# Softmax denominators inverted straight from PSUM and spread by a transpose, with a new table of slots for the attention phase

## The reference

```python
x = L0_attn_q
x = x + 0.5 * _L0_ffn_ref(_layernorm(x), theta, phi, theta_noise, phi_noise)
x = x + _L0_attn_ref(_layernorm(x), Wq, Wk, Wv, Wo)
x = x + 0.5 * _L0_ffn_ref(_layernorm(x), theta, phi, theta_noise, phi_noise)
x = x + 0.5 * _L1_ffn_ref(_layernorm(x), gate_w, gate_b, expert_w, expert_b)
x = x + _L1_attn_ref(_layernorm(x), W_in, A_log, dt_bias, B_norm_bias, C_norm_bias, W_out)
x = x + 0.5 * _L1_ffn_ref(_layernorm(x), gate_w, gate_b, expert_w, expert_b)
```

```python
xq = rope(q @ Wq); xk = rope(kv @ Wk); xv = kv @ Wv
xk, xv = repeat(xk, 2), repeat(xv, 2)
scores = jax.nn.softmax(xq @ xk * scale, axis=-1)
out = (scores @ xv).transpose(0, 2, 1, 3).reshape(batch, seq_len, -1)
return out @ Wo
```

## Time and profile before

| what | value |
|---|---|
| median of 3 runs | 2895.76 us (2888.0 to 2897.27) |
| the profiled execution | 2892.05 us, span of its trace 2890.3 us |
| granted TensorE clock, mean over the span | 0.938 |
| PE matmul busy | 2428.1 us (84%) |
| DVE busy | 1918.0 us (66%) |
| ACT busy | 1465.3 us (51%) |
| POOL busy | 1257.4 us (44%) |
| DVE maxima, L327 | 1024 times, 680 ns each |
| ACT exponentials, L464 | 1024 times, 596 ns each |
| POOL pair sums, L533 | 384 times, 1277 ns each |

### The profile page before, as it was taken

The page is one execution under the profiler, slowest core; times in us unless marked ns, Lnnn a source line. Parts: engine busy times, 40 slices in busy tenths (PEclk is TensorE's granted clock), DMA queues, the critical chain, the costliest instruction groups (busy, mean ns, idle before and its releaser), DMA issues. The chain is left out here.

```text
span 2890.3 us, 41583 instructions
## 1 busy us (share of the span) xinstructions
PE 2428.1 (84%) x14724; PEld 1163.0 (40%) x14724; DVE 1918.0 (66%) x4634; ACT 1465.3 (51%) x2794; POOL 1257.4 (44%) x1104
## 2 busy tenths in 40 slices
PE   2788988898889889988898837999999999997578
PEld 1223332332333233323332224666666666665333
DVE  4776777677777777777777213666666666665477
ACT  2266656655665666566655625555555555552000
POOL 3365556555655655565553412233223223322233
PEclk8799999999999999999999968999999999998789
DMA  2212111111121112111111010000000000000011
GB/s 101 64 32 47 39 36 36 46 34 41 30 52 34 27 44 49 31 31 47 44 27 26 5 45 5 8 12 12 8 9 12 9 11 8 9 5 9 26 51 44
DMA packets 73293, 87.01 MB, mean 30 GB/s; under 512 B 9216, under 2 KB 59520, under 8 KB 72960
## 3 DMA queue, kind: packets, MB, share of 16 engines
q1 hardware_dynamic: 73088, 84.37, 11.6%
HBM read 21.16 MB, written 12.58 MB: 12 GB/s over the span
## 5 line engine op out<-in xcount | busy, mean ns | idle before, releaser
L327 DVE TENSOR_REDUCE mS<-ps 128x1 f32<-128x512 f32 x1024 | 676.2, 680 | 319.4 <-PE ps L670 314.9
L464 ACT ACTIVATE pr<-ps 128x512 f32<-128x512 f32 x1024 | 583.5, 596 | 394.6 <-PE ps L654 383.5
L533 POOL TENSOR_TENSOR prs<-pr 128x512 f32<-128x512 f32 x384 | 484.3, 1277 | 336.5 <-ACT pr L464 336.5
L670 PE MATMUL ps<-kst,qst 96*128 96x512 f16 x1024 | 406.7, 398 | 60.7 <-DVE mS L327 48.3
L654 PE MATMUL ps<-qst,kst 97*128 97x512 f16 x1024 | 400.6, 395 | 47.9 <-ACT pr L464 45.5
L692 PE MATMUL ps<-pr,vt 128*32 128x512 f32 x2048 | 286.1, 632 | 0.1
L654 PEld LDWEIGHTS ps<-qst,kst 97*128 97x128 f16 x1024 | 99.5, 98 | 412.6 <-ACT pr L464 275.2
L537 POOL TENSOR_TENSOR terms<-terms 128x512 f32<-128x512 f32 x128 | 162.2, 1267 | 138.6 <-DVE terms L320 138.6
L320 DVE TENSOR_TENSOR terms<-ps,rope 128x512 f32<-128x512 f32 x256 | 172.5, 676 | 28.0 <-POOL lo L542 22.0
L1396 ACT ACTIVATE m_rl<-m_ps,posb 128x512 f32<-128x512 f32 x128 | 86.1, 684 | 192.2 <-PE m_ps L1682 192.2
L670 PEld LDWEIGHTS ps<-kst,qst 96*128 96x128 f16 x1024 | 101.5, 99 | 197.6 <-DVE mS L327 129.1
(11 more groups left out here) (250 smaller groups left out, 4489.9 us busy)
## 6 DMA issues: line engine op xcount, KB each, us to landing
qst<-hi SPq DMA_DIRECT2D x128, 128.0 KB, 2.4
kst<-hi SPq DMA_DIRECT2D x128, 128.0 KB, 2.4
qst<-lo SPq DMA_DIRECT2D x64, 128.0 KB, 2.4
kst<-lo SPq DMA_DIRECT2D x64, 128.0 KB, 2.4
x<-in_q SPq DMA_DIRECT2D x16, 256.0 KB, 2.7
rope<-in_rope SPq DMA_DIRECT2D x1, 4096.0 KB, 12.2
x<-yold SPq DMA_DIRECT2D x16, 256.0 KB, 2.3
m_x<-x SPq DMA_DIRECT2D x16, 256.0 KB, 2.8
```

The costliest lines, as they stand in the source:

```text
L327: v.tensor_reduce(mS[:, b % 2, t, s:s + 1], ps[:, 2 + n % 2, :], AX, ALU.max).then_inc(S["s_read"], 1)
L464: a.activation(pr[:, s % 2, g, :], ps[:, g % 2, :], ACT.Exp, scale=ATT_SCALE).then_inc(S["exp"], 1)
L533: g.tensor_tensor(prs[:, c, :], pr[:, 0, c, :], pr[:, 1, c, :], ALU.add).then_inc(S["prs"], 1)
L670: mm(ps[:, 2 + n % 2, :], qst[0:3 * DH, h, P * t:P * t + P], kst[0:3 * DH, h, :], start=True, stop=True).then_inc(S["s"], 1)
```

## The change

In the division, the ACT copy is gone: the first transpose reads bank 7 of PSUM itself, and it raises the semaphore `den`, so PE may write the bank again when DVE has read it. The copy that repeated the inverses is gone too: the second transpose reads `inv` with each element repeated 32 times by its access pattern. The multiply gets a wait for the numerators (`o`). The three parts move from slots 24 to 26, 40 to 42 and 56 to 58 to slots 21 to 23, 37 to 39 and 53 to 55; the last group keeps slots 0 to 2. And sixteen numbers of the table change: the four value projections, aggregation of the first norm, both evacuations, ffn, squares, top two and count of the gate, and five of the 16 projections.

```diff
--- before.py
+++ after.py
@@ -71,18 +71,11 @@
 
 ATTENTION_AT = {
 
-
-    "values": (1, 3, 8, 9), "output": 4, "x2": 4,
-
-    "stats1": 5, "aggr1": 9, "xn1": 11, "turn1": 16, "evac1": 16, "ffn": 17, "squares": 21, "ffn_b": 22,
-    "squares_b": 22, "sqrt": 25, "resid": 25, "stats2": 27, "aggr2": 29, "xn2": 31, "turn2": 36, "evac2": 36,
-    "gate": 37, "gate_in": 37, "gate_top": 38, "gate_count": 44,
-
-    "project": (37, 38, 39, 40, 41, 43, 44, 46, 47, 48, 50, 51, 54, 57, 59, 60), "high_lag": 3, "low_lag": 2,
-    "denominators_lag": 3,
-
-
-    "maxima": 5,
+    "values": (0, 1, 7, 8), "output": 4, "x2": 4, "stats1": 5, "aggr1": 8, "xn1": 11, "turn1": 16, "evac1": 17,
+    "ffn": 18, "squares": 19, "ffn_b": 22, "squares_b": 22, "sqrt": 25, "resid": 25, "stats2": 27, "aggr2": 29,
+    "xn2": 31, "turn2": 36, "evac2": 35, "gate": 37, "gate_in": 37, "gate_top": 41, "gate_count": 45,
+    "project": (37, 38, 39, 40, 41, 42, 45, 46, 47, 49, 50, 51, 53, 56, 59, 60), "high_lag": 3, "low_lag": 2,
+    "denominators_lag": 3, "maxima": 5,
 }
 
 HEAD_GROUPS = 6
@@ -337,17 +330,21 @@
                 def divide(b, j, part):
 
                     if part == 0:
+                        if j < NG - 1:
+                            dve.wait_ge(S["dn"], 2 * ((NG - 1) * b + j + 1))
+                        else:
+                            dve.wait_ge(S["dd"], NT * (b + 1))
+                        ins = v.transpose(denT[:, :], ps[:, 7, :])
+                        ins.then_inc(S["den"], 1)
                         dve.wait_ge(S["den"], NG * b + j + 1)
-                        dve.wait_ge(S["dve"], mark(v.transpose(denT[:, :], den[:, :])))
                         div_done[0] = mark(v.reciprocal(inv[:, :], denT[:, 0:SEQ:32]))
                     if part == 1:
                         dve.wait_ge(S["dve"], div_done[0])
-                        dve.wait_ge(S["dve"], mark(v.tensor_copy(
-                            denT[:, :].rearrange("p (b i) -> p b i", i=32),
-                            inv[:, :].rearrange("p (b o) -> p b o", o=1).to_broadcast([P, SEQ // 32, 32]))))
-                        div_done[0] = mark(v.transpose(den[:, :], denT[:, :]))
+                        div_done[0] = mark(v.transpose(
+                            den[:, :], inv[:, :].rearrange("p (b o) -> p b o", o=1).to_broadcast([P, SEQ // 32, 32])))
                     if part == 2:
                         dve.wait_ge(S["dve"], div_done[0])
+                        dve.wait_ge(S["o"], NG * b + j + 1)
                         v.tensor_tensor(oT[:, j, :], oT[:, j, :], den[:, :], ALU.mult).then_inc(S["norm"], 1)
 
 
@@ -360,8 +357,8 @@
                             maximum(maximum_at(i, q))
                         if guard_at(i, q) is not None:
                             guard_row(guard_at(i, q))
-                        if is_att(i) and s % NG == 2 and s > NG and t < 3:
-                            divide(i - 2, s // NG - 1, t)
+                        if is_att(i) and s % NG == 1 and s > NG and t:
+                            divide(i - 2, s // NG - 1, t - 1)
                         if is_old(i) and q < 3:
                             divide(i - 3, NG - 1, q)
                         if is_old(i) and q == AT["x2"]:
@@ -440,15 +437,6 @@
                         act.wait_ge(S["wo"], b)
                     a.copy(oT[:, j, :], ps[:, 6, :]).then_inc(S["o"], 1)
 
-                def denominators(b, j):
-                    if j < NG - 1:
-                        act.wait_ge(S["dn"], 2 * ((NG - 1) * b + j + 1))
-                    else:
-                        act.wait_ge(S["dd"], NT * (b + 1))
-                    if NG * b + j:
-                        act.wait_ge(S["norm"], NG * b + j)
-                    a.copy(den[:, :], ps[:, 7, :]).then_inc(S["den"], 1)
-
                 def exponentials(b, s, g):
                     head = HEADS * b + s
                     if g == 0 and head >= 2:
@@ -475,8 +463,6 @@
                                 a.copy(vt[:, t, :], ps[:, 5, :]).then_inc(S["v"], 1)
                             if s and s % NG == 0 and g == 3:
                                 numerators(i - 2, s // NG - 1)
-                            if s > NG and s % NG == 1 and g == 2:
-                                denominators(i - 2, s // NG - 1)
                         for part in range(4):
                             if q == AT["xn1"] + part:
                                 normalise(i, lambda t: x8[:, t, :], 1, part)
@@ -505,7 +491,6 @@
                             high(i, high_at[q])
                     if is_att(i):
                         numerators(i - 2, NG - 1)
-                        denominators(i - 2, NG - 1)
 
             @block.gpsimd
             def _(pool):
```

## The result

The changed kernel takes 2824.88 us (median of 4 runs, 2820.94 to 2825.83); the kernel before took 2892.53 us beside it (2888.0 to 2897.27). The ratio is 0.976, with a 95% interval of 0.9742 to 0.9778: 2.4% faster. The profiled span fell from 2890.3 to 2824.0 us, by 66.3, at a mean granted clock of 0.944 instead of 0.938. One execution in all that follows, one of the four of e4_actcopy, took 3216.14 us at a mean clock of 0.73; the ratios leave it out.

A forecast was written before the change was run, and what follows sets the result against it. PE was taken as nearest to a bound, yet idle 12 us per iteration, waiting for other engines. Gains of 0.6 + 0.6 + 2.1 + 0.4 = 3.7 us per full iteration, 54 us in all, gave 2840 us, range 2810 to 2880.

The forecast's parts named there:

- the likeliest case: The forecast proper, all four stages gaining as summed: 2824 to 2858 us, chance 0.62.
- T1: Slots 5 to 16, first norm: aggregation one slot earlier, with two maxima ahead of it instead of three; gain 0.6 us.
- T2: Slots 22 to 36, ffn to second norm: the division's multiply leaves DVE's run behind the root; gain 0.6 us.
- T3: Slots 38 to 52, rotary products: shorter division lets POOL's chain start sooner and take 16.0 us; gain 2.1 us.
- T4: Slots 0 to 4, last inverse ahead of the output projection: DVE's copy leaves the chain; gain 0.4 us.
- ACT's copy at nothing: Removing ACT's copy of 0.584 us was priced at gain 0; 0.58 at most in T1 to T4 if ACT were late.
- B: Rival: POOL or ACT takes T3, which then brings 0.1 us; 26 us gained, 2866 us; chance 0.13.
- C: Rival: T3 gives up all its DVE waits, 3.9 us, and the clock comes back; 2799 us; chance 0.07.
- D: Rival, slower: PE's waits at slots 27 and 28 merge, half clock reaches into T3; 2903 us; chance 0.07.
- E: Rival: a new transpose is slow, 1.42 us in place of 0.70; 24 us gained, 2868 us; chance 0.06.
- D's rate: Each us of half clock reaching into T3 would cost about half a us.
- waits for terms: Sign: PE's waits for DVE products, 50.3 us before, fall below 30 us in 13 iterations.

The follow-up runs named there:

- e4_actcopy: Changed kernel with ACT's copy of the denominators put back, the first transpose reading that copy; 2849.99 us, 0.9839 of the kernel before.
- e2_table: New table of slots with the division of the kernel before (both copies, old division slots); 2887.35 us, 0.9973 of the kernel before.
- e5_first_late: Changed kernel with only the first group's division moved back from slots 21 to 23 to slots 24 to 26; 2837.94 us, 0.9821.
- e11: Changed kernel with the gate's choices back in slot 38 and PE's gaps filled by repeated score matmuls; 2831.13 us, 0.9792.
- e10: Changed kernel with one number put back, the gate's choices in slot 38 instead of 41; 2868.35 us, 0.9921 of the kernel before.
- e1: Changed kernel's division (no copies, new slots) with the table of slots of the kernel before; 2878.91 us, 0.9938.
- e9: New division with the table of the kernel before, except the gate's choices in slot 41, not 38; 2847.11 us, 0.9846.
- e3_dvecopy: Changed kernel with DVE's spreading copy put back ahead of the second transpose, which reads the copy; 2863.61 us, 0.9886.
- the filled kernels: Kernels in which PE repeats score matmuls where it stood idle, e11 and i4_fill; 2831.13 and 2812.19 us.
- i4_fill: Changed kernel with the eight score matmuls of slots 26, 27 and 30 to 35 issued three times; 2812.19 us, 0.9719.

## Why the prediction came out as it did

The forecast was 2840 with a range of 2810 to 2880; 2824.9 lies in it, at the lower edge of the likeliest case's own 2824 to 2858. The mechanism was right, and the steady part of the sum was right to 0.05 us. That closeness is in part luck: T1 and T2 together gave 1.06 us and not 1.2, T3 and T4 a little more than forecast.

- **T1, 0.6 predicted.** The first shift stands 7.97 us behind the residual, 8.56 before: 0.59. e2_table shows the same 0.59 alone. At the second ffn 0.46 of it is left.
- **T2, 0.6 predicted, 0 for squares and evacuations.** 0.60 more at the second shift. e5_first_late undoes it and loses 0.60. The squares and evacuations were not tried singly. For the squares PE's rows bear the argument out: behind the second ffn it waited 1.05 us for POOL's pair sum and 0.72 for ACT before, and now waits 0.75 and 1.02, the same 1.77 in all. In the changed kernel:

```profile
727.91 1.07 PE L686 MATMUL ps<-prs,ones 128*32 128x512 f32 x8 [0.75 <-POOL prs L518]
730.00 0.39 PE L639 MATMUL ps<-qst,kst 97*128 97x512 f16 x1 [1.02 <-ACT pr L452]
```

- **T3, 2.1 predicted.** 36.0 to 33.8: 2.2, at full clock. POOL's chain took exactly the 16.0 us worked out, and the multiply fell in POOL's pause and took 0.67, the better of the two cases. One step was wrong all the same: "the table's other shifts (gate_top 38 to 41, ...) leave DVE's sum the same". The sum stays, and yet with gate_top at 38 T3 takes 35.1 us at full clock (e11) and 37.3 with the clock that it then gets (e10). My chain from maximum to product silently had the choices out of slot 38 already; I used the new place and priced it at nothing. Undoing it costs 43 of the 68 us, some 20 by the order and the rest by the clock, and without it the new division brings 0.6% (e1) in place of 1.5% (e9).
- **T4, 0.4 predicted.** The stretch from the last division's first transpose to the output projection fell from 3.83 to 3.38, 0.45. The value projections' wait of 0.24 is hidden, as said.
- **The sum.** 3.7 per iteration against 3.72 between the cleanest iterations, 48.1 against 48.4 in 13.
- **ACT's copy at nothing.** The stages came out right without it, so it held where the copy stood; e4_actcopy shows that it does not hold in the new order.
- **What was missing, 12 us of 66.** Iterations 16 and 17 gave 8.5 and not 3.2; the clock in the 13 iterations gave 3.6 and the phases that the change leaves alone 3.4, which is luck. For iteration 16 I took T1, T2 and T4 and left T3 out because it has no projections. But it has the gate, its choices and counts, and the division.

The kernel before in iteration 16, DVE and then PE in the timeline behind the gate sum of 1546.27:

```profile
1548.40 1.28 DVE L59 CAST gif<-gix 128x8 f32<-128x8 uint32 x1
...
1550.47 0.51 PE L670 MATMUL ps<-kst,qst 96*128 96x512 f16 x1 [1.95 <-DVE mS L327]
1560.95 0.61 PE L670 MATMUL ps<-kst,qst 96*128 96x512 f16 x1 [2.82 <-DVE mS L327]
```

The window of its 18 us from that gate sum on:

```profile
1546.27:1564.27 18.00, 12.92 (x56) 2.73 (x54) 16.28 (x34) 7.22 (x13) 7.42 (x6) 0.81 0.01 1
```

The changed kernel in the same place, behind the gate sum of 1491.13:

```profile
1497.28 0.17 DVE L59 CAST gif<-gix 128x8 f32<-128x8 uint32 x1
...
1503.28 0.39 PE L655 MATMUL ps<-kst,qst 96*128 96x512 f16 x1 [1.66 <-DVE mS L320]
```

Its window of 18 us:

```profile
1491.13:1509.13 18.00, 14.99 (x80) 3.37 (x78) 16.10 (x36) 9.51 (x17) 8.08 (x7) 1.00 0.01 2
```

Before, DVE had choices, division and counts in one run, a cast of 8 columns took 1.28 us beside POOL's pair sums (0.17 now), PE waited up to 2.82 us for the maxima behind it, and the mean clock was 0.81. Now PE gets through 80 matmuls in place of 56, at full clock. e3_dvecopy loses 7.8 us here again, but 3.3 of them are already lost when its gate sum comes. The whole iteration lasts 77.8 and 79.4 us in two profiles of the changed kernel, 81.9 in e10 and 79.2 in e11, so the clock has a part in it; how much is DVE's run and how much the clock was not separated.

**The rivals.** B (POOL or ACT takes T3 and leaves no gain) is refuted: POOL's chain bounds T3 now, but at the shorter length that was counted. C's gain through the clock came in part: 3.6 us; T3 gave 2.2 and not its 3.9. D, the slower case, did not come, as the changed kernel's T3 has a clock of 1.00 in all 13 iterations; but e10 shows its mechanism to be real, 2.2 us per iteration, one table entry away. D's rate holds too: a mean of 0.84 in 22 us is 7 us at half clock, and they cost 2.9 us, a little under half a us each. By the rule of the Trainium skill quoted there ("TensorE: Matmul & The Clock Gate", Part 1), activity releases the clock; the filled kernels agree with it, 2812 against 2826 us. E is refuted by the tiles' 706 and 696 ns. The signs named in the prediction were met but for two: the residuals' distance is 94.0 where 94.3 stood, and the second norm's shift comes 1.06 us sooner where 1.2 stood. The others: waits for terms 22.5 us (below 30), waits for ACT up to 48.1.

What stays open: why a costly fall of the clock comes in about every second iteration of the changed kernel and in every one of e4's and e9's, and why the filled kernels have none. PE's longest wait in an iteration, 1.04 us, is the same in the changed kernel and in i4_fill; that the period of the iteration plays a part is a guess. And e1_code has the division in its new slots: the pure removal of the copies, with both old slots and table, was not tried. By the order of the queues PE would wait there at slot 55 for a bank that DVE gives free only at slot 56; no run shows it.

## What to carry to other kernels

Count a stage as a chain: which engine's result starts it, what stands ahead of that instruction on its queue, and which waits it holds; the busy sum of an engine told nothing here, since 18.2 us of DVE work gave a stage of 33.8 or of 35.2 us at the same full clock. Two edits that free the same chain are to be priced together: alone they brought 0.6% and 0.3%, together 2.4%. Read a stage in every iteration before naming its length: in e1_code and e10_top38 one stage has two or three lengths, set by the clock, and a single one of them misleads. And where the mean iteration is longer than the cleanest, look for PE's idle stretches at the time when the granted clock falls, and try to fill them with repeated work before planning anything larger.
